# Front of a transformer layer on one core: order of splitting and scaling, early entries, row loads and filler products

## The reference

```python
def _L0_attn_ref(x, Wq, bq, Wk, bk, Wv, bv, Wo, bo):     # x: 4 x 1024 x 128, 16 heads of 8
    q, k, v = x @ Wq.T + bq, x @ Wk.T + bk, x @ Wv.T + bv  # then split into heads
    scores = einsum('bhqd,bhkd->bhqk', q, k) / sqrt(8)
    scores = where(tril, scores, NEG)                      # causal
    out = einsum('bhqk,bhkd->bhqd', softmax(scores), v)
    return out.transpose(...) @ Wo.T + bo
def _L0_ffn_ref(x, gate_w, w_gate, w_up, w_down):        # 8 experts, 64 wide, the best one of each token
    sel, rw = argmax(x @ gate_w.T), sigmoid(max(x @ gate_w.T))
    # for each expert e: xs = x * rw * (sel == e); out += ((xs @ w_up.T) * silu(xs @ w_gate.T)) @ w_down.T
x = x + _L0_attn_ref(_layernorm(x), ...)
x = x + _L0_ffn_ref(_layernorm(x), ...)
```

## Time and profile before

| | |
|---|---|
| median of 3 runs | 548.43 us (546.91 to 548.87) |
| profiled execution | 549.08 us, its span 547.3 us |
| mean granted clock of TensorE | 0.981 |
| TensorE busy | 517.4 us (95%) |
| VectorE busy | 467.7 us (85%) |
| ScalarE busy | 384.4 us (70%) |
| GpSimd busy | 208.1 us (38%) |
| split parts of half 1 made | about 22.9 us |
| first piece of unit 0 on TensorE | 33.50 us |
| second piece | 38.39 us |
| first piece of unit 1 | 63.87 us |

### The profile page before, as it was taken

How to read it: one execution, slowest core, us unless ns; L and a number is a source line. 1 busy time by engine, 2 the same in 40 slices (tenths; PEclk the granted TensorE clock), 3 DMA queues, 4 the chain that set the end, 5 groups by cost and what they waited for, 6 DMA issues and landing times.

```text
span 547.3 us, 12283 instructions
## 1 busy us (share of the span) xinstructions
PE 517.4 (95%) x4642; PEld 234.5 (43%) x4642; DVE 467.7 (85%) x701; ACT 384.4 (70%) x771; POOL 208.1 (38%) x390
## 2 busy tenths in 40 slices
PE   7659899999999999999999999999999899999997
PEld 6324434343343433434334333343323366666664
DVE  6938899999999999999999999999982278888864
ACT  7224589898998889889898898988887723333331
POOL 5477264452444534435244453441342221111100
PEclk9769999999999999999999999999998999999999
DMA  6151121510201422011061110211300022221001
GB/s 177 35 168 43 48 65 37 152 50 24 71 17 57 134 55 72 18 56 57 18 180 25 55 50 24 71 36 52 93 4 22 6 83 62 59 59 57 20 20 40
DMA packets 27867, 32.46 MB, mean 59 GB/s; under 512 B 4384, under 2 KB 21280, under 8 KB 27808
## 3 DMA queue, kind: packets, MB, share of 16 engines
q1 hardware_dynamic: 27664, 31.28, 20.0%
q10 hardware_dynamic: 144, 0.39, 0.2%
HBM read 20.26 MB, written 11.01 MB: 57 GB/s over the span
## 4 chain that ended last, share of the span: by engine, by line
PE 62%; DVE 24%; ACT 4%; POOL 4%; issue 4%; DMA 1%; ACTq 1%; POOLq 0%; DVEq 0%
PE ps L1090 19%; PE ps L1074 13%; PE ps L1031 8%; DVE top_p L832 7%; DVE top_p L834 7%; PE ps L1146 5%; ACT prob L688 4%; DVE top_p L827 4%; PE ps L1041 3%; PE ps L1141 3%; PE ps L975 3%; PE ps L1155 2%; PE ps L966 2%; PE ps L1107 1%; DVE xn L765 1%
## 5 line engine op out<-in xcount | busy, mean ns | idle before, releaser
L688 ACT ACTIVATE prob<-ps 128x512 f32<-128x512 f32 (+2 forms) x640 | 307.7, 560 | 47.0 <-PE ps L1074 42.3
L834 DVE TENSOR_REDUCE top_p<-ps 128x2 f32<-128x1024 f32 x192 | 223.6, 1217 | 5.4 <-PE ps L1041 1.8
L1074 PE MATMUL ps<-q_rows,k_rows 51*128 51x512 bf16 (+3 forms) x768 | 169.2, 329 | 2.5 <-ACT prob L688 1.1
L1090 PE MATMUL ps<-prob,v_all 128*9 128x512 f32 (+3 forms) x1536 | 157.0, 489 | 0.6 <-ACT sum_sb L679 0.5
L587 POOL TENSOR_SCALAR_AFFINE_SELECT prob<-prob 128x512 f32<-128x512 f32 x128 | 81.5, 637 | 192.1 <-ACT prob L688 190.6
L1031 PE MATMUL ps<-k_rows,q_rows 48*128 48x512 bf16 (+2 forms) x896 | 130.6, 305 | 9.2 <-DMA k_rows<-split_parts 6.7
L1074 PEld LDWEIGHTS ps<-q_rows,k_rows 51*128 51x128 bf16 x768 | 52.4, 93 | 135.6 <-ACT prob L688 120.2
L832 DVE TENSOR_REDUCE top_p<-ps 128x4 f32<-128x1024 f32 x64 | 76.4, 1215 | 3.5 <-PE ps L1041 3.3
L1031 PEld LDWEIGHTS ps<-k_rows,q_rows 48*128 48x128 bf16 x896 | 42.7, 94 | 45.8 <-issue 15.4
L827 DVE TENSOR_REDUCE top_p<-ps 128x8 f32<-128x1024 f32 x32 | 39.1, 1223 | 14.8 <-PE ps L1041 14.2
L1041 PE MATMUL ps<-shade,pick 64*128 64x128 bf16 (+3 forms) x512 | 50.9, 245 | 0.0
(11 more groups left out here) (86 smaller groups left out, 450.2 us busy)
## 6 DMA issues: line engine op xcount, KB each, us to landing
split_parts<-part SPq DMA_DIRECT2D x6, 768.0 KB, 5.1
q_rows<-split_parts SPq DMA_DIRECT2D x31, 96.0 KB
k_rows<-split_parts SPq DMA_DIRECT2D x31, 96.0 KB
value_sums<-sum_sb SPq DMA_DIRECT2D x128, 18.0 KB
x_sb<-x SPq DMA_DIRECT2D x8, 256.0 KB, 4.5
qk<-value_sums SPq DMA_DIRECT2D x8, 256.0 KB, 3.7
qk<-inverse_sums SPq DMA_DIRECT2D x8, 256.0 KB, 4.3
out<-y SPq DMA_DIRECT2D x8, 256.0 KB, 2.3
```

Source lines behind the costliest of these rows:

```text
L688: a.activation(prob[:, i % NB, g0:g0 + heads, 0:cols], ps[:, load_at(u, n) % 3, 0:heads * cols].rearrange("p (s t) -> p s t", s=heads), AC ...
L834: return v.tensor_reduce(top_p[:, place, qt, s:s + 3:2], banks, AX.X, ALU.max)
L1074: last = mm(ps[:, l % 3, m * cols:(m + 1) * cols], k_rows[rows, k, s + m, j * P:(j + 1) * P], q_rows[rows, k, s + m, c * HALF + q0:(c + 1) ...
L1090: last = mm(ps[32 * g:32 * g + HD + 1, BANK_V, q0:HALF], v_all[:, b, j, first_head + g, :], prob[:, i % NB, g, 0:n], start=(j == 0), stop= ...
```

## The change

VectorE makes the parts of both halves of batch 0 (`take_parts(0)`, `take_parts(1)`) before it scales half (1, 0). On GpSimd the subtraction for part 3 of half 0 goes ahead of the memset of the ones in `v_all`. `AHEAD` becomes 8: q, k and v of half (1, 1) now stand before the first piece, and sixteen entries instead of nineteen are spread over the eighteen pieces, so that the step after the ninth piece (with the turn) and the one after the last have none. In `EARLY`, xn_t of (2, 0) now follows v of (1, 1). ScalarE takes one entry instead of three before it waits for the split parts, and issues four row loads of row group 1 instead of six; the remaining two are SP's, behind its own six. SP waits until all twelve have landed before it sends the other units' parts. TensorE runs 36 filler products into bank 0 between the bias product and the first early entry.

```diff
 for half, after in zip(HALVES, HALVES[1:]):
     EARLY += [("q", *half), ("k", *half)]
-    if after:
+    EARLY += [("v", *half)] if half == (1, 1) or not after else [("xn_t", *after), ("v", *half)]
+    if half == (1, 1):
         EARLY.append(("xn_t", *after))
-    EARLY.append(("v", *half))
-AHEAD = 5
+AHEAD = 8
...
-        def load_half(eng, u, rg):
+        def load_half(eng, u, rg, groups=PART_ROWS):
...
-            for first_row, n in PART_ROWS:
+            for first_row, n in groups:
...
             def load_rows(u):
-                for rg in range(2 if u else 1):
-                    load_half(sp, u, rg)
+                load_half(sp, u, 0)
+                load_half(sp, u, 1, PART_ROWS if u else PART_ROWS[2:])
...
             load_rows(0)
+            sp.wait_ge(rows_in[0], 192)
             for h in range(2):
                 send_parts(0, h, range(1, UPB))
...
             rsqrt1(2, 2)
-            g.memset(v_all[:, :, :, :, HD:HD + 1], 1.0).then_inc(v_ones_set, 1)
             pool.wait_ge(part2_set, 1)
             g.tensor_tensor(part[:, 0, :, 2, :], rest[:, 0, :, :], part[:, 0, :, 1, :],
                             ALU.subtract).then_inc(part3_set[0], 1)
+            g.memset(v_all[:, :, :, :, HD:HD + 1], 1.0).then_inc(v_ones_set, 1)
...
-            for e in EARLY[:3]:
+            for e in EARLY[:1]:
                 take(e)
             for h in range(2):
                 act.wait_ge(split_out[h], 16)
             act.wait_ge(k_rows_set, 1)
-            load_half(act, 0, 1)
-            for e in EARLY[3:]:
+            load_half(act, 0, 1, PART_ROWS[:2])
+            for e in EARLY[1:]:
                 take(e)
...
             take_parts(0)
+            take_parts(1)
             scale(1, 0)
-            take_parts(1)
             scale(1, 1)
...
-            for n in range(64):
-                mm(ps[:, 3, 0:P], ident_b[:], ident_b[:], start=True, stop=True)
+            def keep_busy(times, bank):
+                for n in range(times):
+                    mm(ps[:, bank, 0:P], ident_b[:], ident_b[:], start=True, stop=True)
+            keep_busy(64, 3)
...
             mm(ps[:, 4, 0:DIM], xs[:, 0, 0, :], w_o[:], start=True, stop=True).then_inc(bias_mm, 1)
+            keep_busy(36, 0)
             for e in EARLY[:AHEAD]:
                 early(*e)
```

## The result

| | before | changed |
|---|---|---|
| median | 548.45 us (545.57 to 551.81, 20 runs) | 543.86 us (542.13 to 547.05, 20 runs) |
| profiled execution, its span | 549.08, 547.3 us | 544.17, 542.2 us |
| mean granted clock in it | 0.981 | 0.984 |
| split parts of half 1 made | 22.9 us | 20.6 us |
| first piece of unit 0 | 33.50 us | 31.55 us |

The ratio is 0.9915, 95% interval 0.9898 to 0.9932: 4.6 us faster, where 5.4 us (543.1) were forecast. The number came out near, and partly by luck: two terms inside were off in opposite directions, which gave 6.85 us at the start of unit 0 instead of 5.4, and a third thing, which the sum had left out, took part of that away.

What follows compares the result with a forecast made beforehand. TensorE, busy 95% of the span, bounds the kernel, so front savings pass through. First piece 0.3 us later, less 5.7 to unit 0, gives 5.4 us less: 543.7 profiled, 543.1 median; range 540.0 to 546.7.

Steps and rivals of the forecast that it cites:

- VectorE and GpSimd: Front, parts of half 1: the engines exclude one another, GpSimd's 2.2 us stay in series, second split at 21.0.
- The row loads: Front: eight loads issued by SP, four by ScalarE; last landing 2.5 us after issue, rows in at 31.6.
- The first piece: Unit 0's first piece: stays in place, at 33.4, decided by the eight early entries and not the loads.
- My bound of 32 for being wrong: Sign of error: the first piece of unit 0 starting before 32 (or after 36).
- a wait for GpSimd's xn (2, 0): Sign of error behind the first piece: TensorE waits for this half, forecast ready at 33.3 and wanted at 34.2.
- From there to unit 0: First piece to unit 0's own order: 6.5 us go, some come back, net 5.7 less than 30.37.
- The largest term that goes: Between the first two pieces: q and k of (1, 1) leave, 3.7 us; 1.5 us to the second piece.
- the last v copy: End of the lead: TensorE's 0.85 us wait for it goes, since v (3, 1) stands before the last piece.
- Two that come back: Lead: returning costs were put at 0.3 for xn (2, 0)'s copy, 0.5 for reductions and VectorE's backlog.
- A: Rival, front: first piece moves, through no exclusion (540.9), fillers keeping 2.4 GHz (542.0) or both (539.8); chance 0.28.
- B: Rival, behind the first piece: GpSimd's xn (2, 0) comes at 37.4, TensorE stands 3.2 us, 546.3; chance 0.11.
- C: Rival, front and lead: TensorE doesn't come back to 2.4 GHz; a rise at 50 gives 553; chance 0.05.

Runs made afterwards that it cites:

- e6_vector_part3: Changed kernel with the part 3 subtraction of half 0 on VectorE instead of GpSimd; 542.60 us, 0.9894 of the kernel before.
- e9_no_sp_wait: Changed kernel without SP's wait for the row loads; 543.04 us, 0.9877 of the kernel before.
- e12_with_tail_filler: Changed kernel with VectorE's part 3 subtraction, GpSimd's batch 2 scaled sooner, 94 front fillers, and fillers in the last unit; 542.65 us, 0.9875 of before.
- e3_no_filler: Changed kernel without the 36 filler products; 542.62 us, 0.9894 of the kernel before.
- e8_scale2_sooner: Changed kernel with GpSimd scaling batch 2 ahead of the reciprocal roots of steps 6 and 7; 543.90 us, 0.9911 of the kernel before.
- e2_after_again: Changed kernel run once more without edit, beside the kernel before; 544.34 us, 0.9923 of before.

## Why the prediction held, step by step

**VectorE and GpSimd: right.** 21.0 was forecast for the second split, 20.6 came, with one instruction of take_parts(1) stretched to 3.04 us beside GpSimd's; `e6_vector_part3` takes the cause away and the stretch goes.

**The row loads: right, and 0.7 us sooner than forecast.** 31.6 forecast, 30.86 measured. I let ScalarE issue only when its copy of xn_t was done (23.9). The row of 23.04 shows the issue 0.1 us behind the start of the copy: the DMA's issue doesn't wait for the activation ahead of it. So the copy of q came at 26.42 and not 27.2. That the new wait on SP protects the landing was an expectation that `e9_no_sp_wait` doesn't bear out, and in `e12_with_tail_filler` the loads landed late in spite of it; that it costs nothing held in the profiles.

**The first piece: the term mis-sized.** 33.4 forecast, 31.55 measured. 0.4 are the turn (21.80, not 22.2), the clock came back at 27.5 instead of 28.9, and ScalarE's copies 0.8 sooner. I said "the first piece stays where it is"; it moved by 1.95 us. My bound of 32 for being wrong was passed by it, and the other sign, a wait for GpSimd's xn (2, 0), came too: the time came out right although two signs of being wrong did. The mechanism was right in the profiles of the changed kernel, where the eight entries decided and not the loads; by only 0.7 us, though, and in `e12_with_tail_filler`, whose entries end sooner, a late landing decided. That the fillers cost nothing, and that they bring nothing, `e3_no_filler` bears out in its profile.

**From there to unit 0: 25.47 us against 24.7.** The largest term that goes was right: 1.96 us to the second piece, and 1.25 in `e8_scale2_sooner`, where 1.5 was forecast. Of the 0.85 us for the last v copy only 0.32 went, 0.52 stayed; the forecast had it gone, since v (3, 1) now stands before the last piece, but that copy still ends 0.3 us after that piece. Two that come back were missed or too small: GpSimd's xn (2, 0) was late by 0.68 us, since the first piece was sooner and its own chain (VectorE's measures, the power, 3.14 us of scaling) was not; `e8_scale2_sooner` removes it, for 0.7 us. And at the turn TensorE now waits 0.42 + 0.66 us for reductions: there the lead is VectorE's. I had counted 0.5 for that. These three are 1.8 us too little, and the stretch is only 0.8 us longer than forecast, so some steps were shorter than counted: one is the first piece with its mask, 0.66 us at 2.4 GHz (31.29 to 31.95 in `e8_scale2_sooner`) instead of 1.2 (33.50 to 34.7). The rest isn't accounted for. Both terms together: 6.85 us at unit 0's start, against 5.4.

**From unit 0 to the end: the step that was missing.** I took it for granted that the shift passes through. Through 16 units it does (6.6 us). Behind them the profiled executions differ by a spell of the clock that came and went with the same front (10.2 us, and 3.4 in `e2_after_again`), and the time outside the span is 0.2 to 0.4 us longer in all the kernels with the change (1.9 to 2.1 instead of 1.75 us; why is open). For all executions: at an equal mean clock the spans differ by 3.7 to 3.9 us (0.981 and 0.991), and on average an execution has 14.8 us at 1.2 GHz instead of 19.7, which by the correlation goes with 4.9 x 0.23 = 1.1 us. Together 4.8 to 5.0, near the measured difference of the spans (mean 547.0 to 542.1). This divides the difference but doesn't explain it: by the profiles the change is worth 6.6 us up to the last unit, with the low clock's part in it at most 2.3 by the estimate above. The profiles show 17.1 us of low clock in the front before and 6.8 with the change, so 10 us should have gone and only 5 did: in part longer spells in the last unit, in part executions of before whose front was better than the profiled one. No profile caught such an execution, and how the two share is open.

**Rivals.** A (the piece moves) was in part what happened, at 31.55, but by neither of its mechanisms: the engines do exclude one another, and the clock did fall. B (GpSimd decides) happened with 0.68 us of its 3.2. C (the clock doesn't return) didn't.

## What to carry to other kernels

A front may hide work behind a wait for DMAs only as long as everything that this work needs stands ahead of the wait's own issues: in the profiles the early entries gave 2.8 us, and with the late split, where copies queued behind DMA issues, 3.45 us were lost. Before speeding up an engine, ask who would take the gain next: 104 fillers brought TensorE 2 us by 25 us and nothing at unit 0. And where time and mean clock scatter together, compare kernels at an equal clock or by a point ahead of the scatter, such as the start of a unit, which one profile of each of these kernels gave again within 0.4 us (63.87 and 63.54, 57.02 and 57.07), where medians of six to twelve executions don't resolve 1 us. But take more than one profile: one front had unit 0 at 55.43 and at 56.85, so a single profile shows which wait has gone, and not what that is worth to a microsecond.

## What the runs showed of the hardware

- A VectorE subtraction with two SBUF inputs stands still until a GpSimd subtraction has ended (3.04 instead of 1.23 us), but not for a memset (1.1 us beside the memset of 17.50; 1.22 us at 19.22 in `e3_no_filler`). The Trainium skill, "SBUF — State Buffer", section "Who interferes with whom", says just this of instructions that only write; here it has its rows.
- Casts, with one input, stand still too: 2.49 instead of 0.69 us beside the same GpSimd subtraction in `e3_no_filler`, and 1.33 us beside the memset in `e12_with_tail_filler`. The two engines' programs are the same in `e3_no_filler` and in the changed kernel, so which instruction is hit differs between executions.
- ScalarE's queue issues a DMA 0.1 us after the start of an activation that takes 0.60 us (23.04 and 22.92). A copy behind four such issues starts only when they are through (26.42).
- TensorE's clock fell at 420.0 in a stretch in which the engine was busy 1.36 of 2 us, and stayed at 1.2 GHz while it was busy 9.74 of 10 us. The first part of a run isn't the only place that it falls.
